# Splitting the product with V over two steps, and half of a projection with it

## The reference

```python
x = x + xattn(layernorm(x), ctx)                  # 8 batches x 512 rows x 512, f32
h = layernorm(x)
qkv = (h @ W_qkv + b_qkv).reshape(B, S, 3, 16, 32)        # 16 heads of 32
attn = softmax(einsum('bqhd,bkhd->bhqk', q, k) / sqrt(32))
attn_out = einsum('bhqk,bkhd->bqhd', attn, v)
gate = softmax(h @ W_gate + b_gate); top 2 of 8 experts
moe_out = sum over the two experts of gate * (h @ W_experts[e] + b_experts[e])
x = x + attn_out + moe_out
```

## Time and profile before

| | |
|---|---|
| Median of 3 runs | 1459.54 us (1453.82 to 1528.65) |
| Profiled execution, its own time | 1458.29 us |
| Its span, first to last instruction | 1456.7 us |
| Busy: PE, ACT, DVE | 91%, 62%, 65% of the span |
| Mean granted clock of PE | 0.955 |

### The profile page before, as it was taken

The page is one execution under the profiler, slowest core; times in us unless marked ns, Lnnn a source line. Parts: engine busy times, 40 slices in busy tenths (PEclk is TensorE's granted clock), DMA queues, the critical chain, the costliest instruction groups (busy, mean ns, idle before and its releaser), DMA issues.

```text
span 1456.7 us, 25076 instructions
## 1 busy us (share of the span) xinstructions
PE 1324.4 (91%) x6720; PEld 971.6 (67%) x6721; DVE 945.7 (65%) x2019; ACT 903.1 (62%) x1828; POOL 365.8 (25%) x580
## 2 busy tenths in 40 slices
PE   4989999999789899999999999999997769999997
PEld 4968888888565566565665656656563347777776
DVE  4256878787388877777777777777776734333432
ACT  4123434344258889899888998989997743333332
POOL 0001222221100040111101110011113027677775
PEclk9899999999899999999999999999997679999999
DMA  5004444447645344473454733447336277787774
GB/s 158 1 18 160 171 166 158 165 159 265 247 120 141 80 104 132 89 179 80 89 133 90 187 80 87 125 100 188 76 91 181 16 239 131 130 144 135 134 135 65
DMA packets 101293, 187.43 MB, mean 129 GB/s; under 512 B 27257, under 2 KB 35577, under 8 KB 99939
## 3 DMA queue, kind: packets, MB, share of 16 engines
q1 hardware_dynamic: 69984, 138.86, 33.1%
q0 software_dynamic: 26624, 42.04, 17.2%
q10 hardware_dynamic: 4611, 5.74, 1.4%
HBM read 71.09 MB, written 69.35 MB: 96 GB/s over the span
## 4 chain that ended last, share of the span: by engine, by line
PE 70%; issue 7%; ACT 7%; DMA 7%; DVE 6%; POOL 1%; ACTq 1%; POOLq 0%; SPq 0%; DVEq 0%
PE banks L216 14%; PE banks L218 13%; PE banks L217 13%; PE banks L1042 9%; PE banks L1026 6%; PE banks L1006 6%; ACT plain L732 3%; ACT banks L722 3%; DMA out_dram<-plain,score_bias 2%; DMA plain<-h_rows,score_bias 2%; PE banks L1099 2%; DVE plain L1465 1%; PE banks L894 1%; PE banks L927 1%; DMA plain<-in_L_xattn_Wq_dram 1%
## 5 line engine op out<-in xcount | busy, mean ns | idle before, releaser
L216 PE MATMUL banks<-parts 128*128 128x512 f32 (+6 forms) x1108 | 437.5, 395 | 30.0 <-issue 7.5
L218 PE MATMUL banks<-parts 128*128 128x512 f32 (+6 forms) x1108 | 423.8, 383 | 0.0
L217 PE MATMUL banks<-parts 128*128 128x512 f32 (+6 forms) x1108 | 423.8, 382 | 0.0
L1465 DVE TENSOR_REDUCE plain<-banks 128x1 f32<-128x512 f32 x512 | 329.1, 684 | 74.6 <-PE banks L1006 71.6
L722 ACT ACTIVATE banks<-banks,plain 128x512 f32<-128x512 f32 x512 | 338.7, 662 | 43.0 <-DVE plain L1465 40.6
L732 ACT ACTIVATE plain<-banks 128x1024 f32<-128x1024 f32 x256 | 262.5, 1026 | 40.9 <-PE banks L1026 39.2
L216 PEld LDWEIGHTS banks<-parts 128*128 128x128 f32 (+1 forms) x1108 | 214.4, 193 | 74.8 <-issue 36.5
L218 PEld LDWEIGHTS banks<-parts 128*128 128x128 f32 (+1 forms) x1108 | 214.0, 193 | 40.4
L217 PEld LDWEIGHTS banks<-parts 128*128 128x128 f32 (+1 forms) x1108 | 215.1, 194 | 34.4
L1006 PE MATMUL banks<-parts 96*128 96x512 f32 x512 | 208.9, 446 | 27.3 <-ACT banks L722 26.6
L1026 PE MATMUL banks<-parts 104*128 104x512 f32 x512 | 176.2, 426 | 15.1 <-ACT plain L732 14.0
(11 more groups left out here) (167 smaller groups left out, 1417.6 us busy)
## 6 DMA issues: line engine op xcount, KB each, us to landing
parts<-parts SPq DMA_DIRECT2D x384, 128.0 KB, 2.4
h_turned<-parts SPq DMA_DIRECT2D x32, 512.0 KB, 3.0
parts<-h_turned SPq DMA_DIRECT2D x32, 512.0 KB, 7.2
plain<-in_x_dram SPq DMA_DIRECT2D x32, 256.0 KB, 3.0
out_dram<-plain SPq DMA_DIRECT2D x32, 256.0 KB, 2.0
h_rows<-plain SPq DMA_DIRECT2D x32, 256.0 KB, 2.0
parts<-plain SPq DMA_DIRECT2D x8, 1024.0 KB, 4.6
out_dram<-plain POOLq DMA_DIRECT2D x16, 512.0 KB, 6.2
```

The costliest lines, as they stand in the source:

```text
L216: pe.matmul(out, stat[0], mov[0], start=first, stop=False)
L217: pe.matmul(out, stat[0], mov[1], start=False, stop=False)
L218: return pe.matmul(out, stat[1], mov[0], start=False, stop=last)
L1465: dve.tensor_reduce(nmx[:, k, t:t + 1], bank[SB[t]][:], AX.X, ALU.max, negate=True).then_inc(q["f_max"], 1)
```

## The change

The order on PE of the step with the product ends without `PVb`. In its place it has the first half of the next step's item (`Da@-1`, a negative lag), ahead of `S2`. The step behind it becomes a kind of its own, `PW`: `S0`, then `PVb` (written `PWb`), then `T2@2`, `S1`, `n@1`, `S2`, then only the second half of its item, `S3` and, last, `T0@1`. ACT copies the result out in that step (`PW`, after `E3@1`). In the step with the product DVE empties bank 2 (`D@1`) before it copies the maxima in (`n@1`).

```diff
-        PLAN = ["R0", "PV3", "R1", "R2 OT3", "R3", "PV0", "V0", "V1 OT0", "N0", "PV1", "N1", "N2 OT1", "N3", "PV2", "V2", "V3 OT2"]
+        PLAN = ["R0", "PV3", "R1 PW3", "R2 OT3", "R3", "PV0", "V0 PW0", "V1 OT0", "N0", "PV1", "N1 PW1", "N2 OT1", "N3", "PV2", "V2 PW2", "V3 OT2"]
...
             "dense": {"pe": "S0 S1 T2@2 n@1 S2 Da S3 OT T0@1 Db",
                       "act": "E3@1 t2@2 E0 E1 t0@1 D E2",
                       "dve": "s@1 D@1 m0 n@1 m1 m2 m3 OT"},
-            "PV": {"pe": "T2@2 S0 n@1 S1 S2 PVa S3 T0@1 PVb",
-                   "act": "t2@2 E3@1 E0 E1 t0@1 E2 PV",
-                   "dve": "s@1 n@1 D@1 m0 m1 m2 m3"}}
+            "PV": {"pe": "T2@2 S0 n@1 S1 Da@-1 S2 PVa S3 T0@1",
+                   "act": "t2@2 E3@1 E0 E1 t0@1 E2",
+                   "dve": "s@1 D@1 n@1 m0 m1 m2 m3"},
+            "PW": {"pe": "S0 PWb T2@2 S1 n@1 S2 Db S3 T0@1",
+                   "act": "E3@1 PW t2@2 E0 E1 t0@1 D E2",
+                   "dve": "s@1 m0 n@1 m1 m2 m3"}}
...
-            kind = "PV" if "PV" in work[0] else "dense"
+            kind = work[-1][0:2] if work[-1][0:2] in ("PV", "PW") else "dense"
...
-                elif what[0:2] in ("OT", "PV"):
+                elif what[0:2] in ("OT", "PV", "PW"):
...
-                        elif what == "PV":
+                        elif what == "PW":
                             o_out(of, head)
...
-                        elif what[0:2] == "PV":
+                        elif what[0:2] in ("PV", "PW"):
                             pv(of, head, what[2])
```

## The result

The changed kernel takes 1518.3 us (median of 4 runs, 1516.2 to 1519.8) against 1455.3 for the kernel before: 1.043 times as long, 95% interval 1.040 to 1.046. The 1455.3 leaves out one execution that was in a slower state of the chip and took 1528.7; with it the median of the kernel before is 1457.4. It is slower, as forecast; the forecast was 1512. The profiled execution has a span of 1518.2 us, 61.5 more than before.

A forecast was written before the change was run, and what follows sets the result against it. The prediction took neither PE nor ACT as full: the order, through waits between them, decides. Step orders 17, V0's fetch 27 and the clock 10 sum to 54 us on 1458.3, giving 1512 us; range 1472 to 1540.

The forecast's parts named there:

- V0's wait: In PV0, V0's first half waits on PE for the next batch's tile 0, fetched behind R3: 3.8 us, 27 in all.
- The layout of the steps: New PE orders laid out by hand: cycles 0.57 us longer with R or N items, 0.64 with V, 17 us in all.
- The lost cover of T2: In the OT step, T2 waits 0.9 us for ACT's t0, since T0 now comes last with no PVb or Db behind.
- The clock: PE's 4.6 us pause at V0's wait drops the clock to 0.50: 1.5 us lost each time, 10 in all.
- 1 (the even steps win): Waits of S2 and PVa go as PE's steps even out: 1449 us, or 1472 with half of it; chance 0.17.
- 2 (the tile lands sooner): V0's tile lands in 3.0 us, so the wait is 1.5, too short for the clock: 1486 us; chance 0.08.
- 3 (the clock stays down): Each pause at V0 starts a long low-clock stretch, costing PE 5 us instead of 1.5: 1537 us; chance 0.08.
- 4: V0 doesn't wait, covered by ACT's backlog, and the even steps win too: 1412 to 1440 us; chance 0.04.
- The row against the fit: V0's 512 KB fetch: profile rows say 4.8 to 6.1 us, the skill's fit 3.2 (near 1487 us); the rows decide.

The follow-up runs named there:

- e2: Changed kernel with all its orders, but V0 reads the next batch's tile 0 from its own buffer, filled by one more DMA early in the batch: 1478.9 us (1.017).
- e1: Changed kernel, but PV0 and V0 keep the old order (whole product in one step, whole V0 in the next): 1475.8 us (1.0145).
- e4: Kernel before, with the new order in the cycle of PV0 and V0 alone: 1500.6 us (1.032).
- h2: Changed kernel with the four tile fetches in the order 1, 2, 3, 0, so that V0's tile lands last: 1556.7 us (1.071).
- e5: e2 and e3 together: V0's tile in its own buffer, and T0 ahead of the item's second half: 1469.2 us (1.012).
- f1: Kernel before with only the item's first half moved into the product's step, in the 21 cycles without V0: 1464.8 us (1.0069).
- f2: Kernel before with only PVb moved behind S0 of the next step, whose item stays whole, in all 28 cycles: 1462.8 us (1.0053).
- h1: Changed kernel, but SP issues the fetch of tile 0 alone and the other three only when it has landed: 1518.5 us (1.042).
- g4: Kernel before, with E2 ahead of D on ACT only in the step in front of each product: 1444.8 us against 1454.3 (0.992).
- e3: Changed kernel, but in the step behind the product T0 goes before the item's second half and not last: 1512.1 us (1.040).

## Why the prediction was right, point by point

- **The time.** Forecast 1512 with 54 us for the change; the profiled spans differ by 61.5. Direction, size and causes hold; the three terms were 17, 27 and 10, and measured about 24, 25 and 19. So the stretch lost 68 us, 14 more than forecast, and the forecast is as near as it is partly by luck: 7 us were gained outside the stretch, by nothing that it names (below). The ends of the forecast's own span, 1488 and 1538, don't follow from the bounds given for its terms, which add up to about 1484 and 1545; the measured time lies inside both.
- **V0's wait.** Forecast 3.8 us in the step, 27 in all. Measured 3.87 in the step shown, 26.1 in six and 27.6 with batch 0's, whose wait of 1.55 the forecast had at the full size: its rows on the landing were all from the loop. In e2 PE is idle for 0.40 at the same place (its trace names no engine that it waited for), so the fetch itself adds about 25; V0's first half starts 25.1 us later in the seven batches than in e2. That it is the fetch was shown by e2 (gone with the buffer), e1 and e4 (gone and come with V0's cycle), and h2 (grows with the landing).
- **The layout of the steps.** Counted from T2 at 932.41: PVa forecast at 5.33 - 1.86 = 3.47, measured 3.48; PVb 6.47, measured 6.48; T2 8.33 and 8.34; `n` 9.28 and 9.35; T2 of the OT step 13.0 and 13.19; its S2 14.24 and 14.43. The cycle takes 24.16 us, 0.75 more than the cycle of the earlier trace rows, where 0.57 was forecast. The missing 0.2 lies between `n` and T0: `n` starts 0.07 late, S2 and what follows it lose the rest, and T0 came at 11.38, not 11.18. The forecast gave this restart of PE behind the wait of `n` nothing. In other cycles the layout was further off: e2's N1 is 1.02 longer than before. By e2 the orders cost 24 us instead of 17, a term too small by three tenths. A layout by hand from measured distances was good to 0.2 us in the best case and to 0.45 in the worst, in cycles of 24.
- **The lost cover of T2** was named as the reason of the 0.6 a cycle. e5 gives back 0.35 of e2's 0.90, and f1 and f2 show that the halves cost 0.46 and 0.24 without it. So it was one of the reasons. In the lists of waits the rest shows as waits at the new places, Da's for bank 2 (10.0 us in e2, none before) and T's for ACT or for the copy of the maxima; which of them makes up the 0.46 and the 0.24 is not shown.
- **The clock.** The mechanism was right, the size was not: about 19 us, not 10 (43.9 less the 25 of waiting). The fall at V0's wait is there in each pass, and at the size forecast: V0's cycles are 37.0 us longer than in e2, 12 more than their waits, or 1.7 a batch where 1.5 was taken. What I hadn't forecast is a second fall, in the N1 cycle, in four of the six passes, at 1.6 us each: N1 took 25.96 where e2, with the same orders, took 24.43.
- **The rivals.** 1 (the even steps win) is out: with fetch and clock removed (e2) they still lose 24 us, and e5, the best order tried for them, 17. 2 (the tile lands sooner) didn't come true in the loop, where the landings were 4.7 to 6.3 us; in batch 0 the tile did land in 3.5. 3 (the clock stays down) didn't happen: behind V0's wait it stood at 0.50 for 3.4 or 6.8 us, and for longer only in the last batch, as before. 4 needed a cover for V0's wait and there is none.
- **The row against the fit.** An estimate of 3.2 us for the fetch came from the Trainium skill, "DMA: Bandwidth & Descriptors", section "Anatomy of one DMA — SWDGE (gpsimd) path", and would have given 1487; the runs don't agree with it in the loop. There the fetch took 4.7 to 6.3 us from issue to landing, 4.8 in the step shown, and the rows were right to decide. In batch 0, with POOL idle, it took 3.5, which is near the estimate.
- **Outside the stretch** nothing needs a cause in the change. The stretch ahead of the first PV0 step ends at 441.26 against 444.23, but in h1, with the same orders there, at 445.31, and in h2 at 439.75; the one behind takes 288.54 us before, 284.82 after and 287.55 in e2. The clock has a part in it: ahead of the first PV0 step it stood at 0.50 for 44.4 us before and for 37.5 after. One such stretch, before, is 425.62 to 432.45, where the changed kernel's trace has 1.00. Why the clock differs there no run shows.

## What to carry to other kernels

Before work is moved ahead in a hand-written order, ask what feeds it and when that is issued: the largest term here was a load that the old order hid so well that no list of waits named it. Lay the new order out against distances measured in the trace, with each shared bank as a resource of its own; an even load of the engine counts for nothing if the turnover of a bank sets the pace. And a small reordering at the one place where no Da follows (g4) won 9 us, where the large one lost 63.

## What the hardware showed that I had not expected

- **The clock fell without a long pause.** In the N1 cycle of the changed kernel the two waits before it were 0.70 and 0.45 us, and then PE ran at 0.50 (1.2 GHz) for 3.4 us:

```profile
997.71 0.73 PE L1029 MATMUL banks<-parts 104*128 104x512 f32 x2 [0.70 <-ACT plain L735]
...
998.96 0.63 PE L1009 MATMUL banks<-parts 96*128 96x512 f32 x1 [0.45 <-ACT banks L725]
```
```profile
999.20:1002.60 3.40, 3.40 (x10) 2.52 (x10) 2.40 (x4) 2.68 (x7) 0.00 (x0) 0.50 0.52 119
```

  The same waits stand in e2's N1 cycles (0.71 and 0.45) at a clock of 1.00 throughout. V0's wait isn't needed for such a fall: e1, which has none, shows it in the loop once in an R1 and once in an N1 cycle, behind waits of 0.70 and 0.46. The wait of T2 may be: in e3, which has V0's wait but T0 ahead of `Db`, no N1 cycle of the loop has a fall. What makes the difference between e2 and the changed kernel, perhaps only how the waits fall in time, stays open. Its price, 1.5 us each time (25.96 - 24.43), is shown.
- **A read of 512 KB from DRAM can be delay first, bytes after.** In h1's fetch the first packet of each DMA engine took 2.0 to 2.1 us, all the others together some 1.5, near 365 GB/s; alone or with three more behind it, PE could go on 4.9 us after the issue. Where POOL moved nothing at the time (batch 0) the first packets took 0.16 to 0.79 us and the landing 3.5. Writes of the same size landed in 3.0.
- **A longer pause costs a longer fall, but little more time.** With V0's tile last (h2) the wait was 8.3 us and the mean clock over that cycle 0.84, against 0.94 with 3.9 us: the clock stood at 0.50 for 10.2 us instead of 3.4. Most of the fall lies inside the pause, where PE has nothing to do; beyond the longer wait the cycle lost only 0.4 us more (4.8 less 4.4).
